# Reordering the opening, two border sequences and the start of the last stage of a Mamba block with a mixture of experts

## What is computed

```python
mod = (silu(c) @ wmod).reshape(8, 6, 1, 256)
sa, ca, ga, sb, cb, gb = (mod[:, i] for i in range(6))
ga, gb = sign * max(abs(.), 0.25) of each            # the clamps
h = layernorm(x) * (1 + ca) + sa
# attention part: RMS norm, projection to 2 x 512, causal convolution over 4 tokens, silu
xn = h * rsqrt(mean(h * h) + eps) * norm_w
xi, z = split(xn @ W_in)
xc = silu(conv4(xi) + conv_b)
dt, B, C = split(xc @ W_x);  dt = softplus(dt @ W_dt + b_dt)
state[t] = exp(dt * A) * state[t-1] + dt * xc * B     # 16 states per channel
y = (sum over states of state * C + D_skip * xc) * silu(z)
x = x + ga * (h + y @ W_out)
h = layernorm(x) * (1 + cb) + sb
# experts: the 2 best of 8 per token, softmax weights
out = relu(normed_e @ W1[e] + b1[e]) @ W2[e] + b2[e] + h
x = x + gb * (weighted sum over the 2 experts)
```

## Time and profile before

| | |
|---|---|
| median of 3 runs | 1552.35 us (1552.22 to 1558.31) |
| the profiled execution | 1550.88 us, its span 1549.1 us |
| busy share of the span | TensorE 86%, VectorE 79%, GpSimd 68%, ScalarE 51% |
| chain that ended last, by engine | TensorE 48%, VectorE 16%, GpSimd 13%, ScalarE 10%, issue 9%, DMA 3% |
| costliest group | GpSimd's product u*B, 512 of 1323 ns, 644.5 us |
| next | VectorE's scan, 512 of 1211 ns, 611.2 us |
| mean granted TensorE clock | 0.93 |

### The profile page before, as it was taken

How to read it: one execution, slowest core, us unless ns; L and a number is a source line. 1 busy time by engine, 2 the same in 40 slices (tenths; PEclk the granted TensorE clock), 3 DMA queues, 4 the chain that set the end, 5 groups by cost and what they waited for, 6 DMA issues and landing times.

```text
span 1549.1 us, 26016 instructions
## 1 busy us (share of the span) xinstructions
PE 1324.8 (86%) x8010; PEld 1071.6 (69%) x8010; DVE 1218.7 (79%) x2149; ACT 786.5 (51%) x1385; POOL 1046.6 (68%) x943
## 2 busy tenths in 40 slices
PE   8567776877877998898798799979799999999997
PEld 3245465565565766657566666868799989999997
DVE  3798999999989899999999998988355545555554
ACT  3676767867866786786787687666000000000000
POOL 3585878899989789889999988987433452122222
PEclk9696998989969899999999999989999999999999
DMA  7212111323214344344343333677867797676672
GB/s 221 78 53 83 48 49 56 97 75 88 86 65 136 113 120 128 82 142 143 106 127 110 85 114 109 189 230 230 287 179 202 215 251 213 195 206 195 192 206 79
DMA packets 129345, 216.36 MB, mean 140 GB/s; under 512 B 17948, under 2 KB 74792, under 8 KB 129080
## 3 DMA queue, kind: packets, MB, share of 16 engines
q1 hardware_dynamic: 110376, 183.86, 38.6%
q0 software_dynamic: 16064, 27.62, 7.7%
q10 hardware_dynamic: 2768, 3.21, 0.8%
HBM read 178.34 MB, written 37.22 MB: 139 GB/s over the span
## 4 chain that ended last, share of the span: by engine, by line
PE 48%; DVE 16%; POOL 13%; ACT 10%; issue 9%; DMA 3%; SPq 1%; DVEq 0%; POOLq 0%; ACTq 0%
PE psum L1712 14%; PE psum L1728 13%; POOL dBu L883 9%; DVE w_sb L2013 8%; PE psum L1514 7%; ACT psum L1137 3%; DVE y L2024 3%; PE psum L1523 2%; PE psum L1480 2%; ACT hc L1121 2%; PE psum L1680 2%; PE psum L1667 2%; POOL rows_d L801 1%; POOL gT L732 1%; DVE w_sb L1994 1%
## 5 line engine op out<-in xcount | busy, mean ns | idle before, releaser
L883 POOL TENSOR_TENSOR dBu<-w_sb,brep 128x512 f32<-128x512 f32 x512 | 644.5, 1323 | 34.8 <-issue 16.0
L2013 DVE TENSOR_TENSOR_SCAN w_sb<-psum,dBu 128x512 f32<-128x512 f32 x512 | 611.2, 1211 | 57.5 <-ACT psum L1137 38.1
L1137 ACT ACTIVATE psum<-w_sb,aneg 128x512 f32<-128x512 f32 x512 | 350.4, 692 | 116.9 <-DVE w_sb L2013 114.4
L1514 PE MATMUL psum<-ident,w_sb 128*128 128x128 f32 x2048 | 303.3, 295 | 117.0 <-DVE y L2024 70.0
L1514 PEld LDWEIGHTS psum<-ident,w_sb 128*128 128x128 f32 x2048 | 248.3, 151 | 192.7 <-DVE y L2024 102.9
L870 POOL DMA_INDIRECT out<-dBu,token x59 | 92.3, 1564 | 303.6 <-DVE dBu L2229 152.5
L1121 ACT ACTIVATE hc<-psum,ct 128x512 f32<-128x512 f32 x256 | 175.1, 684 | 102.8 <-PE psum L1514 69.4
L1523 PE MATMUL psum<-ident,hc 128*128 128x128 f32 x1024 | 171.7, 299 | 33.5 <-ACT hc L1121 23.5
L1523 PEld LDWEIGHTS psum<-ident,hc 128*128 128x128 f32 x1024 | 133.0, 154 | 77.5 <-ACT hc L1121 36.5
L2024 DVE SCALAR_TENSOR_TENSOR y<-psum,ct,y 128x512 f32<-128x512 f32 x240 | 174.8, 728 | 12.9 <-PE psum L1514 12.3
L1712 PE MATMUL psum<-xgT,expert_pieces 128*128 128x128 f32 x960 | 113.9, 277 | 0.0
(11 more groups left out here) (274 smaller groups left out, 1757.7 us busy)
## 6 DMA issues: line engine op xcount, KB each, us to landing
brep<-b_d SPq DMA_DIRECT2D x128, 256.0 KB
expert_pieces<-in_W SPq DMA_DIRECT2D x30, 1024.0 KB
win<-in_W SPq DMA_DIRECT2D x29, 1024.0 KB
expert_pieces<-in_W SPq DMA_DIRECT2D x42, 512.0 KB, 5.9
dBu<-rows_d SPq DMA_DIRECT2D x35, 257.0 KB
w_sb<-in_W SPq DMA_DIRECT2D x8, 1024.0 KB
xg<-rows_d SPq DMA_DIRECT2D x22, 257.0 KB, 2.7
h_d<-hmod SPq DMA_DIRECT2D x8, 512.0 KB, 3.1
```

What stands on the lines that cost most here:

```text
L883: nc.gpsimd.tensor_tensor(dBu[:, i % RING, :], u[p][:, c, :], brep[:, s % 4, :], ALU.mult).then_inc(s_dBu, 1)
L1137: nc.scalar.activation(dA[:, i % DA_RING, :], dt[p][:, c, :], ACT.Exp, scale=aneg[:, c, s:s + 1]).then_inc(s_dA, 1)
L1514: last = nc.tensor.transpose(T[:, i // DT, c * P:(c + 1) * P], hs[s % 2][:, c, i * P:(i + 1) * P], ident[:, :])
L2013: nc.vector.tensor_tensor_scan(hs[s % 2][:, c, :], dA[:, i % DA_RING, :], dBu[:, (n * UNITS + i) % RING, :], 0.0, ALU.mult, ALU.add).then_ ...
```

## The change

No instruction's work changes. What moves:

- **Opening.** ScalarE squares before all three gate copies; `p_norm(1)` goes from ahead of the convolutions to ahead of the last silu; the first z copy leaves the prologue, and all four stand in step 0 of sequence 0, behind two exponentials and a wait for the gates' second store; `c_copy` goes ahead of the last logarithm. GpSimd makes `rms(0)` before `ln1(1)`, and `ln1(2,2,2)` in step 5. VectorE adds 1 to the first gate only after `x_stats(1)`, clamps the others after the convolutions, and takes `x_stats(2)` and `(3)` in steps 1 and 2. SP stores the second half of the gates after four broadcasts of B. TensorE has three zero matmuls at the very start, three instead of eight ahead of the transposes, one instead of two after them.
- **Borders into 3 and 7.** `rank` stands behind the border's last sums, `rank_in` behind all of step 0.
- **Sequence 7.** `tile_hin` and `tile_id` of tile 9 go behind a second exponential and a product with C.
- **Last stage.** SP gathers tile 15's rows ahead of tile 14's W1 and of b2. The output projection of the last sequence comes one tile (first half) and one tile (second half) earlier, with VectorE's residual adds.

```diff
@@ SyncE, prologue and body
                 store_h(0)
-                sp.wait_ge(s_modr, 2)
-                sp.dma_start(mod_d[:, 2 * D:6 * D], m8[:, 2 * D:6 * D]).then_inc(s_modst, 16)
-                sp.wait_ge(s_modst, 32)
-                store_h(1)
...
                     load_brep(n, s)
+                    if n == 0 and s == 0:
+                        store_h(1)
+                    if n == 0 and s == 3:
+                        sp.wait_ge(s_modr, 2)
+                        sp.dma_start(mod_d[:, 2 * D:6 * D], m8[:, 2 * D:6 * D]).then_inc(s_modst, 16)
+                        sp.wait_ge(s_modst, 32)
@@ SyncE, epilogue
                 all_w2(7)
+                late_rows(BEGIN + 3)
                 late_w1(BEGIN + 2)
                 sp.dma_start(b2_sb, b2.to_broadcast([P, E * D])).then_inc(s_b2, 16)
-                late_rows(BEGIN + 3)
@@ GpSimd, prologue and body
                 ln1(0, 1, 0)
+                rms(0)
                 ln1(1, 1, 1)
-                rms(0)
                 p_mod(1)
-                ln1(2, 2, 2)
...
+                    if not has_o and s == 5:
+                        ln1(2, 2, 2)
@@ ScalarE, prologue
-                mod_copy(0)
                 for half in range(2):
...
-                mod_copy(1)
-                mod_copy(2)
+                for j in range(3):
+                    mod_copy(j)
                 norm(0)
...
-                act.wait_ge(s_x1st, 16)
-                p_norm(1, xs_of[1], 1, lambda i: slice(TI + i, TI + i + 1))
...
                 silu_first(2)
-                act.wait_ge(s_modst, 32)
+                act.wait_ge(s_x1st, 16)
+                p_norm(1, xs_of[1], 1, lambda i: slice(TI + i, TI + i + 1))
                 silu_first(3)
                 exps_again()
                 xd_copy(0)
-                z_first(0)
                 decay_rates()
...
+                    if half == 1:
+                        c_copy(0, 0)
...
-                c_copy(0, 0)
-                for c in range(1, CH):
-                    z_first(c)
@@ ScalarE, body
-                    if n >= 3 and s == 8:
-                        tile_hin(t if n < 7 else LATE + 1, 0)
...
                     decays(n, p, s, (1,), has_o)
-                    if n in (3, 7) and s == 0:
-                        rank_in(n // 4, XB)
+                    if not has_o and s == 0:
+                        act.wait_ge(s_modst, 32)
+                        for c in range(CH):
+                            z_first(c)
                     times_c_before(n, p, s, 0, has_o)
...
+                    if n == 7 and s in (8, 9):
+                        tile_hin(LATE + 1, s - 8)
...
                     times_c_before(n, p, s, 1, has_o)
+                    if n in (3, 7) and s == 0:
+                        rank_in(n // 4, XB)
@@ TensorE
+            pe.wait_ge(s_id, 1)
+            warm_up(3)
             pe.wait_ge(s_ct, 32)
...
-                warm_up(8)
+                warm_up(3)
                 norm_t(0)
-                warm_up(2)
+                warm_up(1)
...
-                    if n in (2, 6) and s == 15:
-                        pe.wait_ge(s_z, (n + 2) * CH)
-                        rank(n // 4, XB)
...
                     if s > 0:
                         add_up(n, s, 1)
+                    if n in (2, 6) and s == 15:
+                        pe.wait_ge(s_z, (n + 2) * CH)
+                        rank(n // 4, XB)
...
                 second(BEGIN)
+                out_proj(NB - 1, NB, 0)
+                out_proj(NB - 1, NB, 1)
...
-                    if t in (14, 16):
-                        out_proj(NB - 1, NB, t - 14)
-                        out_proj(NB - 1, NB, t - 13)
+                    if t == 15:
+                        out_proj(NB - 1, NB, 2)
+                        out_proj(NB - 1, NB, 3)
@@ VectorE
+                dve.wait_ge(s_x1st, 16)
+                x_stats(1)
                 dve.wait_ge(s_m8, 1)
                 nc.vector.tensor_scalar(m6[:, 1, :], m6[:, 1, :], 1.0, None, ALU.add).then_inc(s_modr, 1)
-                dve.wait_ge(s_x1st, 16)
-                x_stats(1)
...
-                x_stats(2)
-                x_stats(3)
...
+                    if not has_o and s in (1, 2):
+                        x_stats(s + 1)
...
-                    if t == 15:
+                    if t == 14:
                         o_resid_half(NB - 1, 0)
-                    if t == 17:
+                    if t == 16:
                         o_resid_half(NB - 1, 1)
```

31 lines of the change are left out of this document (17 added, 14 removed).

## The result

The changed kernel takes 1531.77 us (median of 4 runs, 1526.92 to 1535.12) against 1552.60 for the kernel before: a ratio of 0.9856, 95% interval 0.9819 to 0.9893. A second comparison, of six runs, gave 1531.92 and 0.9864 (0.9836 to 0.9892). The profiled execution took 1532.31 us, span 1529.8.

The account below looks back on a forecast made before the run. Bounds: a hand-over chain in the opening, VectorE in the scan stage, TensorE in the last. 1550.88 - 4.1 (opening) - 0 (rank) - 6.2 (last stage) = 1540.6, forecast as a 1541.0 us median; range 1535.5 to 1547.0.

Parts of the forecast that it names:

- The rank step: Borders into sequences 3 and 7: moving rank and rank_in gains 0, from 1.5 us lost to 2 gained.
- Rival 1: Borders: the rank's stall really goes, both idle times, 5.6 us; about 1535 us, chance 10%.
- The opening: Start through first scans: a shorter chain, less the statistics' cost, nets 4.1 us, between 1.5 and 5.5.
- The landing at 32.1 becomes 34.2: Opening: the store of sequence 0's h lands 2.1 us later, as mod_d's store ahead of it leaves later.
- I take 6 ... 52: Opening: the gates' second store takes 6 us from issue at 45.8, landing at 52; fourth scan near 57.7.
- rival 2: Opening only moves its wait, gate or h store landing late: opening 0 to 1.5, 1544 to 1547 us, 14%.
- 3.4 us come back: Sequence 0, steps 1 and 2: two statistics of 1.7 us each cost their length on full VectorE.
- The last stage: Tile 15's rows: 4.33 us of TensorE idle time and the half clock behind it go, 6.2 us won.
- Rival 4: Opening: projections run at 1.2 GHz after fewer zero matmuls; opening -2, 1547 us, chance 5%.
- Rival 5: Scan stage: TensorE's granted clock falls, kernel slower than before, 1562 us; chance 3%.

Follow-up runs that it names:

- after_again: The changed kernel, unchanged, measured once more against the kernel before: 1531.92 us, ratio 0.9864.
- no_rank: The changed kernel with TensorE's rank and ScalarE's rank_in back in their old places: 1541.81 us.
- norm_late: The changed kernel with clamps around VectorE's xnT copy, statistics 2 and 3 in the clamps' old place, and p_norm(1) behind xd_copy: 1531.75 us.
- norm_rank: norm_late with TensorE's rank products back in their old early place and ScalarE's rank_in left late: 1535.33 us.
- open_only: The kernel before with only the change's opening part: 1548.17 us.

## Why the prediction missed

**The rank step failed**: "0; from 1.5 lost to 2 gained". It was worth 10 us. The premise was that ScalarE blocks on the same result anyway, so that VectorE "runs one scan further and stops there". Two errors are in it.

First, VectorE did stop where the prediction said, at the first scan of step 1, but not for rank. I put the end of rank at 443.7 by adding all the work ahead of it. On before's time scale (the kernels are 4.6 us apart there) it came at 441.8; 1.4 of the 1.9 us between are the rank products, which ran at full clock. VectorE's wait at that scan ended with GpSimd's product (1.62 us) and no longer with ScalarE, and the scan started 1.6 us earlier than before, where I had it 0.3 later. Of 4.65 us of waiting for ScalarE (3.54, and 1.11 a little later) only 0.27 is left. But GpSimd's products bound VectorE next (waits of 1.62, 0.59 and 1.87 us in after up to step 4), so that the border itself gives 1.3 us in most traces (36.2 to 34.9) and 3.2 at best.

Second, what follows isn't neutral, and this is the larger part. The dip of 4 us at 3.10, in all seven traces of the old order, is gone in nine of thirteen of the new, and the dip of 4.4 at 4.10, in five of seven, is gone in all. On average over the traces sequences 3 to 6 take 7.9 us less in the new order: 4.3 up to sequence 4, 3.3 from 4.8 to 5.4, 0.3 later. The second border adds 0.2 by step 14. Measured were 10 (interval 6.5 to 13.4 on the kernel before), and 6.0 (1.7 to 8.1) for the first border alone. So some two of the 10 us are in no stretch that I can point to, and they lie within the noise. Rival 1 (the stall really goes) had the right sign and half the size, at 10%, and not the mechanism of the larger half.

**The opening**: mechanism right, size probably off: 6.8 us instead of 4.1, with 2.8 to 8.9 as the interval, so that the runs alone don't exclude 4.1; the traces of before and after are 6.8 apart at 113 us.
- "The landing at 32.1 becomes 34.2" failed in this trace. hmod began at 32.4: x_stats(1) ran earlier with the rest, mod_d left only 1.05 us later than before (15.30 against 14.25), and took 2.31 us to land, not 3.20. In the six other traces with this order on ScalarE hmod begins at 33.1 to 34.4. In after_again, the latest, the last silu ends at 36.97 and the fourth scan starts at 57.14, close to my 36.9 and 57.7; there the late projections (23.80) hold the chain as well.
- "I take 6 ... 52" for the gate store: 5.0 (issued at 43.67, ScalarE's copies at 48.68). With both, the fourth scan came 11.6 us sooner, not 7.5. These were the two transfers on which rival 2 rested; both erred to the other side.
- "3.4 us come back": 4.9 by 113 us. VectorE was full, as read; half clocks (0.50 from 80 to 85 us, 0.61 from 95 to 100) came on top.
- The first scan isn't fixed: of nine traces of the new opening it starts at 49.4 to 50.8 us in five and at 52.7 to 53.4 in four. Two of these four are after_again and no_rank, with the slowest first pieces (below); the other two are norm_late and norm_rank. The old opening varies too, from 61.0 to 63.8 in eleven traces, and before's profile is its earliest. The fourth scan starts at 66.7 on average there and at 55.6 in the four traces of the changed opening as it is: 11.1 us.

**The last stage**: right. 6.2 forecast, 7.1 (interval 4 to 9) measured. Idle 4.33 and the half clock behind it went, as the earlier trace rows said, and no other wait came up. What I couldn't see in one profile: half a clock on the last product ahead of them (tile 13's first or tile 12's second, 5.2 to 6.7 us in place of 3.8 or 3.7) stands in 9 of the 10 traces of the old order and in 8 of the 9 of the new one. The kernel before's first profile is the one without it.

**Rival 4 and the rule of the Trainium skill.** The projections ran at full clock in all nine traces of the new opening: 16 pieces in 7.10 or 7.11 us, behind 1.04 us of transposes and two zero pieces; in after the granted clock was 1.00 from 15 to 35 us. And the rows that spoke for the rival show the opposite a little later. TensorE of the kernel before, from its first transposes of states on, with nothing else between them:

```profile
66.55 1.97 PE L1514 MATMUL psum<-ident,w_sb 128*128 128x128 f32 x8 [6.78 <-DVE w_sb L2013]
69.29 1.97 PE L1514 MATMUL psum<-ident,w_sb 128*128 128x128 f32 x8 [0.77 <-DVE y L2021]
73.77 1.97 PE L1514 MATMUL psum<-ident,w_sb 128*128 128x128 f32 x8 [2.51 <-DVE w_sb L2013]
75.53 1.68 PE L1523 MATMUL psum<-ident,hc 128*128 128x128 f32 x8
77.04 1.04 PE L1460 MATMUL psum<-ident,xn 128*128 128x128 f32 x8
```

All of these are products in transpose mode, the sums at L1523 too. Eight of them took 1.97 us up to 75.5 and 1.04 from 77.04 on, and the granted clock is 0.50 up to 76.5 us and 1.00 from 77 on: it rose while TensorE did nothing else. The Trainium skill, "TensorE: Matmul & The Clock Gate", Part 4: PE-mode transpose, says that transposes don't count as busy time for the clock in the same way as other matmuls, and that full clock doesn't engage for them. These rows don't agree with that, and the measurement decides.

**Rival 5** (the scan stage's clock falls) was the mirror image of what happened: the clock there did react to the reordering, for the better.

## What to carry to other kernels

An engine whose in-order list blocks on another's result stops everything queued behind it; move the waiting instruction behind the work that the bound engine needs next, even if the result then comes later. Before writing 0, work out for the place where the bound engine stops next what it will wait for there, and at what clock the work ahead of it runs. Look at two or three profiles of the kernel before: stretches between the same instructions, laid side by side, show which losses are there only sometimes, and a change can be worth the ones that your profile doesn't have. That holds for the comparison too: before's first profile had the earliest first scan of eleven, and no dip at 4.10. Before an engine's work is moved out of the bound's idle time, check that the place it goes to isn't in the bound itself: the two statistics gave back 4 us of 11.

## What the runs showed of the chip

- **The speed of the first pieces goes with the pause before them.** The six zero pieces end near 6 to 7 us; where TensorE then stood idle 0.59, 1.84, 1.92 or 2.04 us before the real ones, these four took 1.96 us, after 2.29 us 3.19, after 2.60 us 3.65, after 2.91 us 3.34, after 3.02 or 3.10 us 3.75. With no zero matmuls at all they took 3.75 in the kernel before and 3.54 to 3.75 in the eleven traces of the old opening. No run separates the pause from the zero pieces themselves: these took 5.46 to 5.49 us in the four fast cases and 4.36 to 5.07 in the five others, so part of these had already run at the faster rate there. GpSimd's constant, for which the real pieces wait, came at 7.55 us in one trace and between 8.78 and 9.01 in eight, fast and slow ones among them. The granted clock doesn't tell them apart: it reads 1.00 from 7.2 to 10.9 us in the kernel before and 0.50 from 9 to 12 in after_again, where the four pieces took 3.75 us each time. In after_again:

```profile
8.98 3.75 PE L1456 MATMUL psum<-w_sb,xgT 128*128 128x512 f32 x4 [3.02 <-POOL xgT L889]
12.66 6.48 PE L1463 MATMUL psum<-w_sb,prod 128*8 128x512 f32 x12
```

- **Short VectorE steps stretch beside a GpSimd operation.** Two of the clamps' twelve short steps, 0.28 us each elsewhere, took 2.40 and 2.39 us in after, each ending 0.15 us behind one of GpSimd's 2.34 us operations of p_mod(1). In all four traces where the clamps stand there (after, after_again, open_only, no_rank) two steps take 2.3 to 2.4 us; in the five other traces of the new opening, where they stand elsewhere, none does. GpSimd's operations aren't slower for it (2.35 us in norm_late, without the clamps beside them). It cost nothing there; VectorE then waited 0.78 us for ScalarE.

```profile
34.66 2.40 DVE L1966 TENSOR_SCALAR gT<-gT 8x256 f32<-8x256 f32 x1
37.10 2.39 DVE L1967 TENSOR_SCALAR gT<-gT 8x256 f32<-8x256 f32 x1
```

```profile
34.57 2.34 POOL L722 TENSOR_TENSOR hmod<-hmod,modp 128x1024 f32<-128x1024 f32 x1 [17.41 <-ACT hmod L1038]
36.99 2.34 POOL L724 TENSOR_TENSOR hmod<-hmod,modp 128x1024 f32<-128x1024 f32 x1
```

- **A dip of TensorE's clock has fixed places.** At 3.10 and at 4.10 it comes at the same step or not at all, in kernels whose openings differ by 14 us, and costs 4.0 us at the one and 3.8 to 4.4 at the other.
- **Transposes alone raised the clock**, from 0.50 to 1.00 between 76.5 and 77 us in the kernel before (above).
- One-column memsets on VectorE take 18 to 25 ns each on average (1.03 us for 58, 4.92 for 195): a delay made of them has to be read from the trace.
